# A conv-and-attention kernel: first pass without experts, last pass without a next image, and the experts' chain in other steps

## The reference, cut to what matters

```python
for each of 8 images x (128 channels, 32 x 32 = 1024 positions):
    x  = group_norm(x) + pos_emb
    sw = sigmoid(conv1(silu(conv3(silu(conv1(x))))))           # spatial weights
    sh = group_norm(x).T                                       # 1024 tokens
    standard = attention(sh, 8 heads of 16)                    # exact softmax
    multi    = two heads of 64, queries from x * sw
    x  = group_norm((silu([standard, multi] @ ff1) @ ff2) @ out) + residual
    t  = x.T
    t  = t + attention(layer_norm(t), 8 heads of 16)           # the tokens' attention
    n  = layer_norm(t)
    t  = t + top-2-of-8 experts(n): gelu(n @ w1 + b1) @ w2 + b2
    out = t.T
```

## Time and profile before

| what | value |
|---|---|
| median of 3 runs | 3337.78 us (3337.1 to 3339.4) |
| the profiled execution | 3336.73 us, of which its span 3334.8 us |
| granted TensorE clock, mean over the span | 0.933 |
| front block, to the first exponential of pass 1 | 128.5 us |
| the loop, first exponential of pass 1 to that of pass 8's tokens and its end | 128.5 to 3190 us |
| last block (experts of image 7) | 3190 to 3334.8 us |

### The profile page before, as it was taken

The page is one execution under the profiler, slowest core; times in us unless marked ns, Lnnn a source line. Parts: engine busy times, 40 slices in busy tenths (PEclk is TensorE's granted clock), DMA queues, the critical chain, the costliest instruction groups (busy, mean ns, idle before and its releaser), DMA issues. The chain is left out here.

```text
span 3334.8 us, 43735 instructions
## 1 busy us (share of the span) xinstructions
PE 2882.7 (86%) x15510; PEld 1211.6 (36%) x15510; DVE 2229.2 (67%) x4251; ACT 1727.6 (52%) x2592; POOL 639.9 (19%) x558
## 2 busy tenths in 40 slices
PE   4889898998889898998989898898989988898945
PEld 1224432263224532263223632254322622344324
DVE  4664876668774786658775687658765687747840
ACT  1355465555555464555555565554555565554613
POOL 3010230104120230103220140102310050102322
PEclk9699898998999898998989899998989999998967
DMA  4004530163103630154201730144301631035324
GB/s 105 1 21 140 113 64 5 49 186 73 27 14 100 159 65 2 52 166 84 37 14 54 193 65 13 41 131 101 64 9 45 186 73 27 14 122 137 64 73 141
DMA packets 171571, 252.50 MB, mean 76 GB/s; under 512 B 26323, under 2 KB 80287, under 8 KB 171215
## 3 DMA queue, kind: packets, MB, share of 16 engines
q1 hardware_dynamic: 162127, 230.65, 27.3%
q0 software_dynamic: 9216, 18.89, 2.2%
HBM read 192.59 MB, written 56.86 MB: 75 GB/s over the span
## 5 line engine op out<-in xcount | busy, mean ns | idle before, releaser
L1336 DVE TENSOR_REDUCE blockmax<-ps 128x1 f32<-128x512 f32 x1728 | 1135.5, 684 | 397.8 <-PE ps L705 389.2
L1150 ACT ACTIVATE prob<-ps 128x1024 f32<-128x1024 f32 x1024 | 996.2, 1021 | 527.9 <-PE ps L880 518.5
L705 PE MATMUL ps<-ks,qs 96*128 96x512 bf16 x1728 | 688.6, 414 | 200.1 <-DVE blockmax L1336 127.7
L880 PE MATMUL ps<-qs,ks 99*128 99x512 bf16 x2048 | 631.7, 400 | 5.4 <-ACT prob L1150 4.5
L705 PEld LDWEIGHTS ps<-ks,qs 96*128 96x128 bf16 x1728 | 165.4, 102 | 860.2 <-DVE blockmax L1336 655.6
L1195 ACT ACTIVATE prob<-ps,b1t 128x128 f32<-128x128 f32 x828 | 236.7, 369 | 205.4 <-PE ps L983 203.2
L896 PE MATMUL ps<-prob,va_b 128*32 128x512 f32 x2048 | 287.0, 634 | 5.3 <-ACT prob L1150 5.3
L880 PEld LDWEIGHTS ps<-qs,ks 99*128 99x128 bf16 x2048 | 197.5, 102 | 247.2 <-issue 65.5
L896 PE MATMUL ps<-prob,va_a 128*32 128x512 f32 x2048 | 286.5, 633 | 0.0
L589 POOL TENSOR_TENSOR rs<-vn,vec 128x1 f32<-128x1 f32 (+1 forms) x43 | 42.9, 997 | 1253.7 <-DVE vn L1281 884.7
L1347 DVE TENSOR_REDUCE blockmax<-ps 128x2 f32<-128x1024 f32 x192 | 225.4, 1221 | 45.9 <-PE ps L743 44.9
(11 more groups left out here) (229 smaller groups left out, 3344.6 us busy)
## 6 DMA issues: line engine op xcount, KB each, us to landing
shared<-in_w SPq DMA_DIRECT2D x108, 256.0 KB, 3.1
prob<-in_w SPq DMA_DIRECT2D x108, 256.0 KB, 3.3
parts_dram<-parts SPq DMA_DIRECT2D x34, 768.0 KB, 4.8
ks<-parts_dram SPq DMA_DIRECT2D x204, 128.0 KB, 4.2
qs<-parts_dram SPq DMA_DIRECT2D x204, 128.0 KB, 6.3
routed<-in_w SPq DMA_DIRECT2D x90, 256.0 KB, 3.4
xe<-in_w SPq DMA_DIRECT2D x54, 256.0 KB, 3.1
oatt<-in_w SPq DMA_DIRECT2D x54, 256.0 KB, 3.1
```

The source lines that it names most:

```text
L705: pe.matmul(ps[:, MX + n % 2, :], qs[0:ROWS, slot, h, tile * P:(tile + 1) * P], ks[0:ROWS, slot, h, cols(k)], start=True, stop=True).then_ ...
L880: mm = pe.matmul(ps[:, SC + h, :], ks[:, slot_of(a, g), h, t * P:(t + 1) * P], qs[:, slot_of(a, g), h, cols(q)], start=True, stop=True)
L1150: act.activation(prob[:, n % 3, 2 * pr:2 * pr + 2, :], ps[:, SC + 2 * pr:SC + 2 * pr + 2, :], ACT.Exp, scale=HD ** -0.5).then_inc(exp_done ...
L1336: dve.tensor_reduce(blockmax[:, unit_of(j), cell_of(j), k:k + 1], ps[:, MX + n % 2, :], AX.X, ALU.max).then_inc(blocks_used[f], 1)
```

## The change

The loop runs passes 2 to 7 only. Pass 1 is a copy of the code before the loop, without the experts, their routing, and `res` (`without_experts`); pass 8 is a copy behind it, without the next image's front and `a0` blocks (`without_front`). In all passes the routing chain's steps in `CONV_WINDOW` and the counts of `CONV_BLOCKS` change, DVE takes two more blocks before `norm_e` waits for POOL's power, `post` stands ahead of `tg2`, `tg4` moves behind the first early pair, and 4 blocks move from pairs in the scores' banks to the first steps of the tokens' attention.

```diff
-B_EARLY = 48
+B_EARLY = 44
-CONV_WINDOW = {0: ["turn_a1_1"], 1: ["tro0"], 2: ["tro1"], 3: ["tro2"], 4: ["tro3"], 7: ["trn0"], 8: ["trn1"],
+CONV_WINDOW = {0: ["turn_a1_1"], 1: ["tro0"], 2: ["tro1"], 3: ["tro2"], 4: ["tro3"], 8: ["tra0"], 9: ["trn0"],
...
-CONV_EXTRA = {5: ["stats_e"], 6: ["norm_e"], 11: ["routes"], 17: ["gates"]}
+CONV_EXTRA = {5: ["stats_e"], 7: ["norm_e"], 15: ["routes"], 21: ["gates"]}
-EXPERT_WINDOW = {1: ["ff1"], 2: ["ff2"], 3: ["outp"], 4: ["tg2", "post"], 7: ["tr_x"], 8: ["tg3"], 10: ["tr_nb"],
-                 11: ["kB"], 12: ["tg4", "qB"], 13: ["vB"], 17: ["tg5"], 25: ["turn_b_0"]}
+EXPERT_WINDOW = {1: ["ff1"], 2: ["ff2"], 3: ["outp"], 4: ["post"], 5: ["tg2"], 7: ["tr_x"], 8: ["tg3"], 10: ["tr_nb"],
+                 11: ["kB"], 12: ["qB"], 13: ["vB"], 14: ["tg4"], 17: ["tg5"], 25: ["turn_b_0"]}
-CONV_BLOCKS = (4, 3, 3, 3, 3, 0, 1, 5, 5, 4, 0, 1) + (6, 4, 3, 2, 3, 4, 5, 5) + (4,) * 8 + (0,) * 4
-TOKEN_BLOCKS = (5, 4, 4, 3) + (4,) * 8 + (5, 5, 5, 5, 4, 4, 4) + (5, 5, 5, 5, 6, 6) + (5, 5, 5, 6, 6, 5) + (0,)
+CONV_BLOCKS = (4, 3, 3, 3, 3, 1, 3, 2, 4, 4, 2) + (4, 3, 4, 2, 3, 5, 5, 4, 2) + (4,) * 8 + (0,) * 4
+TOKEN_BLOCKS = (5, 5, 5, 5) + (4,) * 8 + (5, 5, 5, 5, 4, 4, 4) + (5, 5, 5, 5, 6, 6) + (5, 5, 5, 6, 6, 5) + (0,)
-ROWS_PAIR = 6
+BETWEEN_PAIRS = {0: "tg4", 7: "tg5", TURN_PAIR: "turn_b_0"}
-UNDER_EXPERTS = SLOT_PAIRS * (SLOTS - PAIR_SLOT)
...
+    blocks = turns_of(TOKEN_BLOCKS, [("b", j) for j in range(B_EARLY, HEAD_BLOCKS)] + late)[n]
+    return [b for b in blocks if front or b[0] == "b"]
...
+def without_experts(name):
+    return not name.startswith(LAST_NORM + ("tg", "res"))
+
+
+def without_front(name):
+    return name.startswith(("turn_b", "res"))
...
         def early_banks(d):
 
-            if d < UNDER_EXPERTS:
-                return pair() if d % 2 else ps[:, MX:MX + 2, :]
-            at = (SC, SC + 2, MX)[(d - UNDER_EXPERTS) % 3]
-            return ps[:, at:at + 2, :]
+            turned = sum(at < d for at in BETWEEN_PAIRS)
+            return pair() if (d + turned) % 2 else ps[:, MX:MX + 2, :]
...
+                before = d - 1 if d - 1 in BETWEEN_PAIRS else d - 2
+                if before >= 0:
+                    pe.wait_ge(blocks_used["b"], 2 * (before + 1))
...
+                elif a == 1 and experts:
+
+                    pe.wait_ge(gelu_done, NC * TILES)
+                    pe.wait_ge(y_used, GROUPS)
                 elif a == 1:
 
-                    pe.wait_ge(blocks_used["b"], B_EARLY)
+                    pe.wait_ge(mexp_done, STEPS)
...
             def layer_norm(src, name):
+                reduce_next()
+                reduce_next()
                 dve.wait_ge(done[f"ln_rstd_{name}"], 1)
...
-        with nc.Fori(0, NB, hint_back_edge=True) as img:
+        run_block(0, True, False, True, True,
+                  Windows(conv=only(CONV_WINDOW, without_experts), parts=only(PARTS_WINDOW, without_experts),
+                          expert=only(EXPERT_WINDOW, without_experts), token=only(TOKEN_WINDOW, without_experts)))
+        with nc.Fori(1, NB - 1, hint_back_edge=True) as img:
             run_block(img, True, True, True, True,
                       Windows(conv=CONV_WINDOW, parts=PARTS_WINDOW, expert=EXPERT_WINDOW, token=TOKEN_WINDOW))
+        run_block(NB - 1, True, True, True, False,
+                  Windows(conv=CONV_WINDOW, parts=PARTS_WINDOW, expert=EXPERT_WINDOW,
+                          token=only(TOKEN_WINDOW, without_front)))
```

More of the change, by code:

```diff
@@ L555, in sync_program @@
                 spread_max("b", 1)
+            if token and not front:
+                spread_max("b", 2)
+                spread_max("b", 3)
             if front:
@@ L634, in pool_program @@
                 rstd("ln_rstd_b", NT)
-                gather_rows()
+                if experts:
+                    gather_rows()
+                if experts and not front:
+                    combine_rows()
             if front:
-                if not token:
+                if not (token and experts):
                     rstd("pre_rstd", 1)
@@ L645, in pool_program @@
                                            ALU.subtract).then_inc(done[f"{x}3_a"], 1)
-                if token:
+                if token and experts:
                     combine_rows()
@@ L889, in weigh_values @@
                     pe.wait_ge(o_taken[a], n // NT)
-                elif t == 0 and a == 0:
+                elif t == 0 and a == 0 and experts:
                     pe.wait_ge(last_taken, 1)
@@ L1013, in tensor_program @@
                             d = SLOT_PAIRS * (s - PAIR_SLOT) + i
-                            if d < UNDER_EXPERTS:
-                                early_pair(d)
-                            if d in (ROWS_PAIR, TURN_PAIR):
+                            early_pair(d)
+                            if d in BETWEEN_PAIRS and (experts or d == TURN_PAIR):
                                 pe.wait_ge(blocks_used["b"], 2 * d)
-                                small_product("turn_b_0" if d == TURN_PAIR else "tg5")
-                if token:
-                    for d in range(UNDER_EXPERTS, B_EARLY // 2):
-                        early_pair(d)
+                                small_product(BETWEEN_PAIRS[d])
                 if not token:
@@ L1161, in scalar_program @@
                         small_product(name)
-                    if n == 12:
+                    if n == 17 and experts:
                         act.wait_ge(done["gate_diff"], 1)
@@ L1177, in scalar_program @@
                         small_product(name)
-                act.activation(warm[:, :], half_b[:, 0:1], ACT.Gelu).then_inc(warmed, 1)
+                if experts:
+                    act.activation(warm[:, :], half_b[:, 0:1], ACT.Gelu).then_inc(warmed, 1)
                 act.wait_ge(mpv_done, STEPS)
-            if experts:
+            if experts or token:
                 for s in range(SLOTS):
@@ L1186, in scalar_program @@
                             small_product(name)
-                    if 1 <= s <= TILES:
+                    if experts and 1 <= s <= TILES:
                         i = s - 1
@@ L1629, in attention_step @@
                     small_product(name)
-            if experts:
+            if experts or conv:
                 late = []
@@ L1636, in vector_program @@
                     names = small.conv.get(n, ())
-                    attention_step(n, late + CONV_EXTRA.get(n, []), names[:-1])
+                    attention_step(n, late + (CONV_EXTRA.get(n, []) if experts else []), names[:-1])
                     late = list(names[-1:])
@@ L1685, in vector_program @@
                 start_xh()
-            if front:
+            if front or token:
                 late = []
-                stream.extend((n, b) for n in range(2 * STEPS) for b in token_blocks(n, token))
+                stream.extend((n, b) for n in range(2 * STEPS) for b in token_blocks(n, token, front))
                 for n in range(2 * STEPS):
@@ L1691, in vector_program @@
                     late_now = [x for x in names[-1:] if x != "turn_a0_0"]
-                    attention_step(n, late + (TOKEN_EXTRA.get(n, []) if token else []),
+                    attention_step(n, late + (TOKEN_EXTRA.get(n, []) if token and front else []),
                                    names[:len(names) - len(late_now)])
```

80 lines of the change are left out of this document (37 added, 43 removed).

## The result

| what | before | after |
|---|---|---|
| median of 4 runs | 3337.46 us | 3233.68 us (3231.3 to 3237.1) |
| ratio to before | | 0.9684, 95% interval 0.9664 to 0.9705 |
| the profiled execution, its span | 3336.73, 3334.8 us | 3235.0, 3233.2 us |

The change is faster by 104 us, 3.2%. The direction was forecast. The time is 44 us above the 3190 forecast: it lies inside the wide range of 3150 to 3250, but outside the 3160 to 3225 that the prediction gave to its own sum.

A forecast was written before the change was run, and what follows sets the result against it. It took PE as busiest (86%), stalled by the experts' routing chain in the image's attention. Six loop passes 66, pass 8 51 and pass 1 31 gave 148 us off 3334.8, plus 3: 3190 us, own range 3160 to 3225, wide 3150 to 3250.

The forecast's parts named there:

- The new table and pairs: Passes 2 to 8: new step table of the image's attention, new pairs and experts' order, together forecast at 78 us.
- parts 4 and 5: Pass 8 without the next image: -39 us in its tokens' attention, -51 in all; pass 1 without experts: -31.
- part 1: Image's attention, passes 2 to 8: reordered routing chain removes PE's stalls, -9 us per pass, between -3 and -13.
- with one wait of about 1 us at `slots`: Image's attention, steps 14 to 16: PE waits once, as `routes` ends behind the last block of step 16.
- the 2 us for `slots` and `gates` in denser steps: Image's attention: both come later, where blocks are dense, and cost 2 us more than before.
- in every second pass the clock falls once more and it is 3 us longer: Image's attention: addition to its step sum of 107.5 us, set against 115 before, giving -9 us.
- parts 2 and 3: Experts' stage reordered: -3 us per pass (-5 to 0); four blocks moved into the tokens' attention: +1 (-2 to +2).
- the stalls only move: Rival, chance 0.12: late small products stop PE in other steps; loop passes gain 2 us each, 3254 us.
- signs of being wrong: New PE waits at `slots` or `trn0`, image's attention clock under 0.94, or PE waits in the copies the profile doesn't explain.
- Part 6: Straight copies' instructions cost no more than the loop's code, which is fetched anew in every pass.
- its rival: Straight copies' instructions come late: at 25 ns each the kernel is slower, 3403 us; chance 0.02.

The follow-up runs named there:

- e1: Kernel before with only the two straight copies (pass 1 without experts, pass 8 without the next image), old tables and pairs: 3250.2 us, ratio 0.9737.
- e5: Kernel before with only pass 1 as a straight copy without experts, loop over passes 2 to 8, old tables and pairs: 3295.7 us, ratio 0.9874.
- e6: Kernel before with only pass 8 as a straight copy without the next image, loop over passes 1 to 7, old tables and pairs: 3298.7 us, ratio 0.9874.
- e7: Changed kernel with `slots` one step later (17) and `qm0` and `qm1` moved to steps 16 and 18: 3215.6 us, ratio 0.9623.
- e9: e7 with DVE's tile biases `b1t` also moved from step 21 to step 28, where no block is left: 3181.2 us, ratio 0.9530.
- e4: Changed kernel plus five useless matmuls on PE around the last values' matmuls at each pass's end: 3229.9 us, ratio 0.9684.
- e11: Changed kernel with the old table of the image's attention, plus five useless matmuls at each pass's end: 3267.6 us, ratio 0.9778.
- e10: e9 plus useless matmuls on PE: 16 ahead of the tokens' first scores and 5 around each pass's end: 3165.1 us, ratio 0.9479.
- e12: e10 with the old pairs and the old order of the experts' products: 3166.4 us, ratio 0.9471.
- the square: Four kernels with both copies: old table with old pairs 3250.2 us, with new pairs 3283.9; new table with old pairs 3225.9, with new pairs 3233.7.

## Why the prediction was right, and where not

**The time: inside the wide range partly by luck.** The new table and pairs were to give 78 us in passes 2 to 8 and gave some 15; the copies were to give 70 and gave 90 (e1). Without those 20 us, which no term has, the same kernel would stand near 3254, past the end of the range.

**Pass 8 and pass 1 (parts 4 and 5): right.** 35.0 for 39 in the tokens' attention of pass 8, with the last 12 steps at 1.9 to 2.6 us, 2.2 in the mean, for 2.1; its other stages gave 1.0 where 11 or 12 stood, which is part 1's failure once more. 33.4 for 31 in pass 1, where the chain alone runs at a clock of 0.69 over the stretch and of 0.5 from 289 to 306 and 316 to 351 us. e1, e5 and e6 show that these two copies are nearly all of the result.

**The image's attention (part 1): the step that failed.** Its first half held. Steps 5 to 8 took 12.4 us where the prediction had 7 off 19.2, so 12.2; steps 12 to 15 took 14.5 for 20.8 before: the two stalls of the earlier trace rows are gone. The sum failed at "with one wait of about 1 us at `slots`" and at the 2 us for `slots` and `gates` in denser steps. The wait is there (1.30 us), but I priced it as a wait alone: the clock falls behind it. And the sum has no term for `b1t`: moving `slots` three steps later carried its tail of 2.4 us on DVE out of the single blocks and in between two multi pairs, where PE waits for each reduction. Steps 16 to 22 came to cost 5.9 us more than before. This is shown: e7 and e9 take the waits at `slots`, `qm1` and `b1t` away, give 7.3 us back in these steps and reach a stage of 111.0 us, the very length that the prediction gave it. In the traces each loop pass is then 7.2 us shorter, 43 us in six, which covers the 37 by which the loop passes fell short.

**The clock at the pass's start: in no term.** The prediction's "in every second pass the clock falls once more and it is 3 us longer" gives its 9 us only if it is read of the kernel before (115 - 107.5 = 7.5, and half of 3); read of the changed kernel the sum would be 6. Read either way, it names no fall at the barrier. There it fell, in passes 3, 4, 6, 7 and 8, for 4.0 + 5.2 us in the first two steps where 2.5 + 3.1 were to be had. That the idle time at the pass's end has a part in it is supported by e4 and e11 (a fill there, and none of passes 2 to 8 starts low). It is not shown to be the whole cause: the fill removes 0.66 us of idle time and leaves the 1.7 of the barrier, it moves the pass's end as well, and in e10 and e12 the clock falls there in spite of it. That this is what coupled table and pairs is shown in part: the fill gives back 16 of 34 us in e11. With both fills the pairs' price is gone (e10, e12), but with the waits in the stage gone too, so which of these did it is open.

**The pairs (parts 2 and 3): small as said, the sign by luck.** The wait did pass to SP's load, and the tokens' blocks cost 1.2 us for 1.5. But a term of 2 us per pass, from parts with ends of -5 to 0 and -2 to +2, can't be told apart from what the clock does to a pass whose length shifts by 2 us. In the square this part cost 8 to 34 us, not gained 14.

**The rival "the stalls only move"** forecast 3254. Of the mechanisms this was the nearer one for the loop: gain 4.8 per pass, between its 2 and the forecast's 11. It gave no place; `routes` behind a block was one of its two reasons, and was one of the places. Two of the prediction's own signs of being wrong came true: a new wait of PE at `slots`, and a clock under 0.94 in the image's attention (0.92 in pass 6). And where it had no step of the image's attention over 5 us, steps 16, 17 and 20 of pass 3 take 6.7, 5.7 and 5.3.

**Part 6** (code costs nothing) was right against its rival: no stretch of the copies has PE waiting for what the profile doesn't show. It missed that the loop's jump got cheaper.

## What to carry to other kernels

When a product with a long tail on another engine is moved, follow the tail, too: ask what work stands between its pieces at the new place, and whether the other engine waits for that work singly or through a double buffer. Price a wait of PE with the clock that falls behind it: waits of 1 to 2 us cost 3 to 4 here. And where a change shifts a pass's length by less than such a fall costs, time its parts in a square before trusting a sum; a fill of useless matmuls over the known gaps is a cheap way to take most of the clock out of the comparison; look in the trace for where it is still low.
